# The last eight experts of a mixture of experts add into one target instead of two, and the other sum is added from on chip

## The chip, the core and the metric

The kernel runs on one core of one Trainium2 chip. The core's engines work side by side: PE (TensorE, matmuls and transposes), DVE (VectorE), ACT (ScalarE), POOL (GpSimd) and SP (SyncE), which here only issues transfers. 16 DMA engines move data between HBM and the on-chip memory (SBUF); all transfers share them, whichever engine issues them. The metric is the device time of one execution in microseconds; smaller is better.

## The reference

The program is two layers of gated attention and feed-forward over 4 x 512 tokens of width 512. The change concerns its last part, a mixture of 64 experts: each token takes its best 8 experts, each expert works on at most 128 tokens, and each token's result is the weighted sum over its experts.

```python
x = x + tanh(g_xattn[0]) * L0_xattn(layernorm(x), ctx)
x = x + tanh(g_ffn[0]) * L0_ffn(layernorm(x))
x = x + tanh(g_xattn[1]) * L1_xattn(layernorm(x), ctx)
x = x + tanh(g_ffn[1]) * L1_ffn(layernorm(x))

def L1_ffn(hidden_states):                 # E, K, F, CAP = 64, 8, 192, 128
    scores = softmax(xf @ router_w.T)
    topk_w, topk_idx = top_k(scores, K)
    topk_w = topk_w / (topk_w.sum(-1) + 1e-20)
    xb = buf[:E * CAP].reshape(E, CAP, h)  # each expert's tokens
    gate = einsum('ech,ehf->ecf', xb, w_gate)
    up = einsum('ech,ehf->ecf', xb, w_up)
    yb = einsum('ecf,efh->ech', silu(gate) * up, w_down)
    slot_out = yb[dest] * topk_w
    return zeros((T, h)).at[slot_token].add(slot_out)
```

## The kernel before

The stages of both layers run one after the other. The last, `layer1_ffn`, first runs `route`, which decides for each expert which rows it takes (`slots`, 128 row numbers for each of the 64 experts) and writes a table of normalised token rows with their weights (`token_table`, in HBM). Meanwhile the ring of expert weights is filled: `ring` holds 17 experts (`RING_E`), 6 KB for gate and up and 4 KB for down a partition each, and expert e lies in slot e % 17. `out` already holds x, the residual, 2048 rows of 512 and 128 spare rows; `second` (`second_sum` in the trace, 2176 rows too) is a tensor of the same shape in HBM that was set to zero long before.

`experts` then runs the 64 experts e = 0 .. 63. For each:
- GpSimd gathers the expert's 128 token rows from the table into `xg` (line 2619), four experts ahead (`AHEAD`).
- PE turns them (line 2672), multiplies by gate and up (2682), turns the product h (2690) and multiplies by down (2699); ACT copies and takes the tanh; DVE builds h (2719, 2721).
- DVE scales the result by each row's weight into `yw` (2727), which has four buffers.
- GpSimd scatters `yw` back with an indirect DMA that adds in flight (line 2629): even experts into `out`, odd ones into `second`.

Two adding transfers into the same rows of one tensor must not be in flight together, so a scatter waits for the landing of the previous scatter into the same target, that is the one two experts before (semaphores `scattered[0]` and `scattered[1]`, 16 for each landing). In GpSimd's order expert e has: wait for `scaled`, gather e + 4, wait for the earlier scatter, scatter e. SP loads the weights of expert e (three transfers, lines 2755 and 2756) once expert e - 17 has finished with their slot.

When both targets' last scatters have landed, GpSimd adds `second` to `out` with four adding transfers from HBM to HBM (line 2635), 512 rows of `out` each, in which every one of 128 descriptors is a run of 2048 floats, 8 KB. Then the kernel ends.

Of the kernel before, what the change touches and what calls it, by code (L numbers as in the profile page):

```python
# [13 lines left out]
ALU = mybir.AluOpType  # L14
# [12 lines left out]
D = 512  # L27
KC = D // P
NT = S // P
T = B * S  # L30
# [46 lines left out]
class Stage:  # L77
# [7 lines left out]
    def sb(self, name, shape, dt):  # L85
        return self.ctx.enter_context(self.nc.sbuf_tensor(f"{self.name}_{name}", shape, dt))
# [4 lines left out]
    def sem(self, name):  # L91
        made = self.nc.semaphore(f"{self.name}_{name}")
        if any(word in name for word in self.OF_DMAS):

            self.kept.append(made)
            return made.__enter__()
        self.sems.append(self.ctx.enter_context(made))
        return self.sems[-1]
# [2178 lines left out]
E = 64  # L2277
# [3 lines left out]
OUT_ROWS = T + CAP  # L2281
# [297 lines left out]
AHEAD = 4  # L2579
RING_E = 17  # L2580
PARTS = 4
W_EXPERT = 2 * KC * F1 + 2 * D
SHARED_E = 6


def experts(nc, table, out, second, slots, wgu, wd, w_loaded, load, c):

    with ExitStack() as ctx:
        st = Stage(nc, ctx, "e1")
        sb, ps, sem = st.sb, st.ps, st.sem  # L2590
# [5 lines left out]
        yw = sb("yw", [P, AHEAD, D], F32)  # L2596
# [3 lines left out]
        y_ps = [ps(f"y_ps{i}", [P, D], F32) for i in range(2)]  # L2600
        names = ("x_turned x_copied gu_done tanhed h_begun h_made h_turned h_copied y_done scaled")
        s = {n: sem(n) for n in names.split()}
        sum_stored = sem("sum_stored")
        scattered = [sem(f"scattered{i}") for i in range(2)]
        gathered = [sem(f"gathered{i}") for i in range(AHEAD)]

        with nc.Block() as block:

            @block.sync
            def _(sp):  # L2610
                for e in range(RING_E, E):
                    sp.wait_ge(s["y_done"], e - RING_E + 1)
                    load(sp, e)

            @block.gpsimd
            def _(pool):
                def gather(e):
                    if e < E:
                        pool.indirect_dma_start(xg[:, e % AHEAD], None, table[:],  # L2619
                                                bass.IndirectOffsetOnAxis(ap=slots[:, e:e + 1], axis=0),  # L2620
                                                bounds_check=OUT_ROWS - 1, compute_op=ALU.bypass).then_inc(gathered[e % AHEAD], 16)
                for e in range(AHEAD):
                    gather(e)
                for e in range(E):
                    pool.wait_ge(s["scaled"], e + 1)
                    gather(e + AHEAD)
                    if e >= 2:
                        pool.wait_ge(scattered[e % 2], 16 * (e // 2))
                    pool.indirect_dma_start((out, second)[e % 2][:], bass.IndirectOffsetOnAxis(ap=slots[:, e:e + 1], axis=0), yw[:, e % AHEAD], None,  # L2629
                                            bounds_check=OUT_ROWS - 1, compute_op=ALU.add).then_inc(scattered[e % 2], 16)  # L2630
                for i in range(2):
                    pool.wait_ge(scattered[i], 16 * (E // 2))  # L2632
                for n in range(PARTS):
                    part = [a[n * T // PARTS:(n + 1) * T // PARTS].rearrange("(p t) n -> p (t n)", t=4) for a in (out, second)]
                    pool.dma_start(part[0], part[1], accum_op=ALU.add, max_dma_last_dim=8192).then_inc(sum_stored, 16)  # L2635
                pool.wait_ge(sum_stored, 16 * PARTS)

            @block.scalar
# [73 lines left out]
            @block.vector  # L2712
            def _(dve):
                def inner(e):
                    i = e % 2
                    dve.wait_ge(s["tanhed"], e + 1)
                    if e >= 2:
                        dve.wait_ge(s["h_turned"], e - 1)
                    dve.scalar_tensor_tensor(h[:, i], th[:, i], 1.0, gu_ps[i][:, 0:F1], ALU.add, ALU.mult).then_inc(s["h_begun"], 1)  # L2719
                    dve.wait_ge(s["h_begun"], e + 1)  # L2720
                    dve.scalar_tensor_tensor(h[:, i], h[:, i], 0.5, gu_ps[i][:, F1:2 * F1], ALU.mult, ALU.mult).then_inc(s["h_made"], 1)

                def scale(e):
                    dve.wait_ge(s["y_done"], e + 1)
                    if e >= AHEAD:
                        dve.wait_ge(scattered[e % 2], 16 * ((e - AHEAD) // 2 + 1))
                    dve.tensor_scalar(yw[:, e % AHEAD], y_ps[e % 2][:], xg[:, e % AHEAD, D + e:D + e + 1], None, ALU.mult).then_inc(s["scaled"], 1)  # L2727

                for e in range(E + 1):
                    if e < E:  # L2730
                        inner(e)
                    if e:
                        scale(e - 1)
# [5 lines left out]
def layer1_ffn(nc, d, x_in, out, second, moments, rows_stored, c):  # L2739

    with ExitStack() as ctx:
        st = Stage(nc, ctx, "m1")
        slots = st.sb("slots", [P, E + 2], U32)
        ring = st.sb("ring", [P, RING_E, W_EXPERT], F32)
        wgu = ring[:, :, 0:2 * KC * F1].rearrange("p r (i k f) -> p r i k f", i=2, k=KC)
        wd = ring[0:FP, :, 2 * KC * F1:].rearrange("p r (c n) -> p r c n", c=2)
        w_loaded = [st.sem(f"w_loaded{u}") for u in range(RING_E)]
        table = nc.dram_tensor("token_table", (OUT_ROWS, ROW), F32, kind="Internal").ap()
        gu_src = [d[n].rearrange("e (p k) f -> e p k f", p=P) for n in ("w_gate", "w_up")]
        d_src = d["w_down"].rearrange("e (p c) n -> e p c n", p=FP)  # L2750

        def load(eng, e):
            u = e % RING_E
            for i in range(2):
                eng.dma_start(wgu[:, u, i], gu_src[i][e]).then_inc(w_loaded[u], 16)
            eng.dma_start(wd[:, u], d_src[e]).then_inc(w_loaded[u], 16)

        route(nc, d, x_in, table, out, slots, ring, load, moments, rows_stored, c)
        experts(nc, table, out, second, slots, wgu, wd, w_loaded, load, c)
        st.clear()  # L2760
def rotary_tables():

# [75 lines left out]
```

## Time and profile before

| | us |
|---|---|
| median of 3 runs | 2864.15 |
| lowest and highest run | 2855.6 and 2873.57 |
| profiled execution, its own time | 2868.23 |
| its span in the profile | 2866.4 |

The page of the profile gives these shares over the whole span: PE 2607.9 us busy (91%), its weight loads 2100.1 us, DVE 1695.4 us (59%), ACT 1291.3 us (45%), POOL 857.9 us (30%). They are averages over stages with different limits. The expert stage takes the last 420 us or so. The rows that matter here come from four views: windows (busy time of every engine in a stretch, with the granted clock of TensorE as a fraction of its full 2.4 GHz and the busy share of the 16 DMA engines), the chain of work that ended last (each piece was released by the one above it), the timeline of one engine (start, duration, in brackets the idle time before and what ended it) and the landing times of the DMAs of one line (from issue until the semaphore says that the data has landed). A share of the DMA engines may read a little over 1, since packets overlap.

### The profile page before, as it was taken

What the parts mean: (1) busy time and instruction counts of PE and PEld (TensorE: products, weight loads), DVE (VectorE), ACT (ScalarE), POOL (GpSimd) and SP (SyncE); (2) the same over time, 40 slices, a digit from 0 to 9 for tenths busy, and PEclk for the clock granted to TensorE, in tenths of its full rate; (3) what the DMA queues carried; (4) which work ended last, traced back from release to release, by engine and by line L of the source; (5) the groups of instructions that cost most, each with busy time, mean ns of one, the idle gap of its engine ahead of it and who ended that gap; (6) DMA issues with size and microseconds to landing.
All of it is one profiled execution on the core that took longest, in us unless ns stands there. A gap on an engine that the chain in (4) does not pass through costs nothing. (4 is left out here: it accounts for less than half of the span.)

```text
span 2866.4 us, 48638 instructions
## 1 busy us (share of the span) xinstructions
PE 2607.9 (91%) x17264; PEld 2100.1 (73%) x17291; DVE 1695.4 (59%) x3810; ACT 1291.3 (45%) x3417; POOL 857.9 (30%) x852
## 2 busy tenths in 40 slices
PE   7999987799999899998999999999999983698895
PEld 5666754699998688887888888888888873355552
DVE  6767687834344766665766666667666657222221
ACT  4777776222123444444655555555555541121221
POOL 3344322000000555554322222222222220344443
PEclk9999998799999999999999999999999996899997
DMA  3110022300012555557512421421241118999976
GB/s 137 45 46 24 20 71 64 101 30 16 30 38 90 179 192 188 178 187 240 172 45 88 141 67 53 144 67 48 83 122 45 38 52 280 257 292 287 291 184 112
DMA packets 227279, 340.06 MB, mean 119 GB/s; under 512 B 24801, under 2 KB 111201, under 8 KB 226529
## 3 DMA queue, kind: packets, MB, share of 16 engines
q1 hardware_dynamic: 209728, 293.56, 32.6%
q0 software_dynamic: 14912, 39.85, 6.6%
q10 hardware_dynamic: 2400, 3.55, 0.4%
q8 instruction: 140, 2.29, 0.3%
q14 instruction: 99, 0.80, 0.1%
HBM read 230.56 MB, written 110.53 MB: 119 GB/s over the span
## 5 line engine op out<-in xcount | busy, mean ns | idle before, releaser
L2058 POOL TENSOR_SCALAR a_prob<-a_prob,a_rinv 128x640 f32<-128x640 f32 (+3 forms) x256 | 253.6, 991 | 741.6 <-DVE a_rinv L2220 741.6
L2210 DVE TENSOR_REDUCE a_mx<-a_s_ps 128x1 f32<-128x640 f32 (+3 forms) x256 | 262.1, 1024 | 247.9 <-PE a_s_ps L2130 241.9
L2082 ACT ACTIVATE a_probT<-a_t_ps 128x512 fp32r<-128x512 f32 (+3 forms) x512 | 237.6, 516 | 346.7 <-PE a_t_ps L2138 346.7
L2226 DVE TENSOR_TENSOR a_probT<-a_t_ps,a_probT 128x512 fp32r<-128x512 f32 (+3 forms) x512 | 276.6, 582 | 45.8 <-ACT a_probT L2082 45.1
L2073 ACT ACTIVATE a_prob<-a_s_ps,a_nb,a_rs 128x640 f32<-128x640 f32 (+3 forms) x256 | 267.9, 1047 | 9.6 <-DVE a_nb L2211 9.6
L137 PE MATMUL a_o_ps<-a_probT,a_v 128*128 128x256 f32 x832 | 245.3, 295 | 0.0
L139 PE MATMUL a_o_ps<-a_probT,a_v 128*128 128x256 f32 x832 | 232.6, 280 | 0.0
L138 PE MATMUL a_o_ps<-a_probT,a_v 128*128 128x256 f32 x832 | 232.4, 279 | 0.0
L2138 PE MATMUL a_t_ps<-kept_ident,a_prob 128*128 128x128 f32 x1664 | 225.2, 274 | 2.6 <-POOL a_prob L2058 2.6
L2138 PEld LDWEIGHTS a_t_ps<-kept_ident,a_prob 128*128 128x128 f32 x1664 | 194.2, 141 | 25.7 <-POOL a_prob L2058 3.2
L736 PEld LDWEIGHTS a_bank<-kept_ident,a_prob 128*128 128x128 f32 x1024 | 114.3, 145 | 121.5 <-ACT a_prob L580 94.1
L736 PE MATMUL a_bank<-kept_ident,a_prob 128*128 128x128 f32 x1024 | 164.1, 290 | 41.4 <-ACT a_prob L580 33.4
L580 ACT ACTIVATE a_prob<-a_prob,a_nmax 128x512 f32<-128x512 f32 x256 | 182.2, 717 | 9.1 <-DVE a_nmax L842 9.1
L2719 DVE SCALAR_TENSOR_TENSOR e_h<-e_th,e_gu_ps 128x192 f32<-128x192 f32 x64 | 22.6, 354 | 272.7 <-ACT e_th L2662 272.7
L2682 PE MATMUL e_gu_ps<-m_ring,e_xT 128*128 128x384 f32 x512 | 180.7, 496 | 1.4 <-ACT e_xT L2645 1.4
L1750 ACT ACTIVATE p_sq<-p_bank 128x128 f32<-128x128 f32 x384 | 101.2, 279 | 154.7 <-PE p_bank L139 154.7
L842 DVE CUSTOM_DVE_ANT_0 a_prob<-a_bank,a_mask 128x512 f32<-128x512 f32 x256 | 161.4, 686 | 12.9 <-PE a_bank L720 12.0
L2682 PEld LDWEIGHTS e_gu_ps<-m_ring,e_xT 128*128 128x128 f32 x512 | 99.6, 195 | 86.5 <-issue 35.2
L138 PEld LDWEIGHTS a_o_ps<-a_probT,a_v 128*128 128x128 f32 x832 | 157.0, 189 | 4.9
L137 PEld LDWEIGHTS a_o_ps<-a_probT,a_v 128*128 128x128 f32 x832 | 156.7, 188 | 5.3
L139 PEld LDWEIGHTS a_o_ps<-a_probT,a_v 128*128 128x128 f32 x832 | 156.3, 188 | 0.0
L2619 POOL DMA_INDIRECT e_xg<-token_table,m_slots x64 | 68.1, 1064 | 276.8 <-DVE e_yw L2727 182.8
(307 smaller groups left out, 7136.2 us busy)
## 6 DMA issues: line engine op xcount, KB each, us to landing
m_ring<-in_w_gate SPq DMA_DIRECT2D x64, 384.0 KB, 6.0
m_ring<-in_w_up SPq DMA_DIRECT2D x64, 384.0 KB, 7.5
m_ring<-in_w_down SPq DMA_DIRECT2D x64, 384.0 KB, 10.7
l_q_hi<-p_turned SPq DMA_DIRECT2D x64, 256.0 KB, 2.4
l_q_lo<-p_turned SPq DMA_DIRECT2D x64, 256.0 KB, 2.1
h_split<-l_q_hi SPq DMA_DIRECT2D x62, 256.0 KB, 3.2
h_split<-l_q_lo SPq DMA_DIRECT2D x62, 256.0 KB, 3.8
l_v_hi<-p_vs SPq DMA_DIRECT2D x32, 256.0 KB, 2.2
```

The source lines that it names most:

```text
L137: pe.matmul(out, ll, rh, start=first, stop=False, **kw)
L138: pe.matmul(out, lh, rl, start=False, stop=False, **kw)
L139: return pe.matmul(out, lh, rh, start=False, stop=last, **kw)
L580: act.activation(prob[:, n % RING0], prob[:, n % RING0], ACT.Exp, bias=nmax[:, n % RING0:n % RING0 + 1], scale=-1.0, accum_out=rsum[:, T % ...
L736: mm = pe.transpose(turn_ps[n % 2][:, a * P:a * P + P], prob[:, n % RING0, a * P:a * P + P], c["ident"][:])
L2058: pool.tensor_scalar(prob[:, k % 4, 0:w], prob[:, k % 4, 0:w], rinv[:, k % 4:k % 4 + 1], 1.0, ALU.mult, ALU.mult).then_inc(s["weighted"], 1)
L2073: act.activation(prob[:, k % 4, 0:w], s_ps[:, k % 2, 0:w], ACT.Exp, bias=nb[:, k % 4:k % 4 + 1], scale=rs[:, u, h:h + 1], accum_out=rsum[: ...
L2082: act.activation(probT[0][:, pair % 2, i * 4:i * 4 + n, k % 2], t_ps[i][:, 0:n * P].rearrange("p (m n) -> p m n", n=P), ACT.Copy).then_inc ...
L2138: mm = pe.transpose(t_ps[i][:, m * P:m * P + P], prob[:, k % 4, (i * 4 + m) * P:(i * 4 + m + 1) * P], c["ident"][:])
L2210: step(dve.tensor_reduce(mx[:, k % 4:k % 4 + 1], s_ps[:, k % 2, 0:w], AX.X, ALU.max))
L2226: dve.tensor_tensor(probT[1][:, pair % 2, i * 4:i * 4 + n, k % 2], t_ps[i][:, 0:n * P].rearrange("p (m n) -> p m n", n=P), probT[0][:, pai ...
L2682: mm = pe.matmul(gu_ps[e % 2][:, 0:2 * F1], xT[:, e % 2, k], wgu[:, u, :, k], start=(k == 0), stop=(k == KC - 1))
```

## The change

The experts from 56 on (`ALTERNATING`) all scatter into `out`; `target(e)` names the target and `nth(e)` counts how many scatters went to it before. SP gets two waits and four transfers behind its last weights: once expert 50 has finished and all 28 scatters into `second` have landed, it loads `second` (without its spare rows) into slots 13 to 16 of the ring, viewed as `sums`. GpSimd's last four adding transfers read from `sums` and not from `second`, and wait for the loads too.

```diff
@@ -2579,11 +2579,13 @@
 AHEAD = 4
 RING_E = 17
 PARTS = 4
+ALTERNATING = 56
+SUM_SLOT = 13
 W_EXPERT = 2 * KC * F1 + 2 * D
 SHARED_E = 6
 
 
-def experts(nc, table, out, second, slots, wgu, wd, w_loaded, load, c):
+def experts(nc, table, out, second, slots, wgu, wd, w_loaded, load, c, ring):
 
     with ExitStack() as ctx:
         st = Stage(nc, ctx, "e1")
@@ -2600,7 +2602,17 @@
         y_ps = [ps(f"y_ps{i}", [P, D], F32) for i in range(2)]
         names = ("x_turned x_copied gu_done tanhed h_begun h_made h_turned h_copied y_done scaled")
         s = {n: sem(n) for n in names.split()}
-        sum_stored = sem("sum_stored")
+        sum_stored, sum_loaded = sem("sum_stored"), sem("sum_loaded")
+        sums = ring[:, SUM_SLOT:SUM_SLOT + 4].rearrange("p r n -> p (r n)")[:, 0:PARTS * 4 * D].rearrange("p (c n) -> p c n", c=PARTS)
+
+        def target(e):
+            return 1 if e % 2 and e < ALTERNATING else 0
+
+        def nth(e):
+            return e // 2 if e < ALTERNATING else ALTERNATING // 2 + e - ALTERNATING
+
+        def part(a, n):
+            return a[n * T // PARTS:(n + 1) * T // PARTS].rearrange("(p t) n -> p (t n)", t=4)
         scattered = [sem(f"scattered{i}") for i in range(2)]
         gathered = [sem(f"gathered{i}") for i in range(AHEAD)]
 
@@ -2611,6 +2623,10 @@
                 for e in range(RING_E, E):
                     sp.wait_ge(s["y_done"], e - RING_E + 1)
                     load(sp, e)
+                sp.wait_ge(s["y_done"], ALTERNATING - 5)
+                sp.wait_ge(scattered[1], 16 * (ALTERNATING // 2))
+                for n in range(PARTS):
+                    sp.dma_start(sums[:, n], part(second, n)).then_inc(sum_loaded, 16)
 
             @block.gpsimd
             def _(pool):
@@ -2625,14 +2641,13 @@
                     pool.wait_ge(s["scaled"], e + 1)
                     gather(e + AHEAD)
                     if e >= 2:
-                        pool.wait_ge(scattered[e % 2], 16 * (e // 2))
-                    pool.indirect_dma_start((out, second)[e % 2][:], bass.IndirectOffsetOnAxis(ap=slots[:, e:e + 1], axis=0), yw[:, e % AHEAD], None,
-                                            bounds_check=OUT_ROWS - 1, compute_op=ALU.add).then_inc(scattered[e % 2], 16)
-                for i in range(2):
-                    pool.wait_ge(scattered[i], 16 * (E // 2))
+                        pool.wait_ge(scattered[target(e)], 16 * nth(e))
+                    pool.indirect_dma_start((out, second)[target(e)][:], bass.IndirectOffsetOnAxis(ap=slots[:, e:e + 1], axis=0), yw[:, e % AHEAD], None,
+                                            bounds_check=OUT_ROWS - 1, compute_op=ALU.add).then_inc(scattered[target(e)], 16)
+                pool.wait_ge(scattered[0], 16 * (nth(E - 1) + 1))
+                pool.wait_ge(sum_loaded, 16 * PARTS)
                 for n in range(PARTS):
-                    part = [a[n * T // PARTS:(n + 1) * T // PARTS].rearrange("(p t) n -> p (t n)", t=4) for a in (out, second)]
-                    pool.dma_start(part[0], part[1], accum_op=ALU.add, max_dma_last_dim=8192).then_inc(sum_stored, 16)
+                    pool.dma_start(part(out, n), sums[:, n], accum_op=ALU.add, max_dma_last_dim=8192).then_inc(sum_stored, 16)
                 pool.wait_ge(sum_stored, 16 * PARTS)
 
             @block.scalar
@@ -2723,7 +2738,7 @@
                 def scale(e):
                     dve.wait_ge(s["y_done"], e + 1)
                     if e >= AHEAD:
-                        dve.wait_ge(scattered[e % 2], 16 * ((e - AHEAD) // 2 + 1))
+                        dve.wait_ge(scattered[target(e - AHEAD)], 16 * (nth(e - AHEAD) + 1))
                     dve.tensor_scalar(yw[:, e % AHEAD], y_ps[e % 2][:], xg[:, e % AHEAD, D + e:D + e + 1], None, ALU.mult).then_inc(s["scaled"], 1)
 
                 for e in range(E + 1):
@@ -2756,7 +2771,7 @@
             eng.dma_start(wd[:, u], d_src[e]).then_inc(w_loaded[u], 16)
 
         route(nc, d, x_in, table, out, slots, ring, load, moments, rows_stored, c)
-        experts(nc, table, out, second, slots, wgu, wd, w_loaded, load, c)
+        experts(nc, table, out, second, slots, wgu, wd, w_loaded, load, c, ring)
         st.clear()
 def rotary_tables():
```

The order of instructions changes in two places. The first is GpSimd's end, from the scatter of expert 55 on (`L2629` before is `L2645` now, the gather `L2619` is `L2635`; tiles `e_yw` are the scaled results, `m_slots` the row numbers). Before:

```order
 L2629 DMA second_sum<-e_yw,m_slots 2176x512
 L2619 DMA e_xg<-token_table,m_slots 128x576
 L2629 DMA out_rows<-e_yw,m_slots 2176x512
 L2619 DMA e_xg<-token_table,m_slots 128x576
 L2629 DMA second_sum<-e_yw,m_slots 2176x512
```

Changed:

```order
 L2645 DMA second_sum<-e_yw,m_slots 2176x512
 L2635 DMA e_xg<-token_table,m_slots 128x576
 L2645 DMA out_rows<-e_yw,m_slots 2176x512
 L2635 DMA e_xg<-token_table,m_slots 128x576
 L2645 DMA out_rows<-e_yw,m_slots 2176x512
```

Nothing is moved in GpSimd's stream; every second scatter has another target, and the last four transfers another source.

The second is the end of SP's queue, behind the loads of expert 63 (`m_ring` is the ring):

```order
+L2770 DMA m_ring<-in_w_gate 128x768
+L2770 DMA m_ring<-in_w_up 128x768
+L2771 DMA m_ring<-in_w_down 96x1024
+L2629 DMA m_ring<-second_sum 128x2048 x4
+L2619 UNCONDITIONAL_BRANCH
```

The four loads of the second sum stand last on that queue, with nothing behind them.

## Rows read from the trace of the kernel before

**Rows 1.** windows by stage, core 0; x counts instructions, PEclk is the granted clock

```profile
core 0: us, PE busy (x) PEld busy (x) DVE busy (x) ACT busy (x) POOL busy (x), PEclk, DMA share, GB/s
5.00:25.00 20.00, 14.07 (x56) 11.54 (x57) 12.90 (x22) 8.12 (x11) 4.05 (x5) 1.00 1.04 373
2500.00:2700.00 200.00, 179.49 (x598) 101.96 (x596) 48.10 (x99) 39.95 (x100) 88.60 (x68) 0.97 1.05 289
2752.00:2818.00 66.00, 66.00 (x229) 38.15 (x228) 18.06 (x38) 15.58 (x39) 34.20 (x26) 1.00 0.58 111
2841.00:2861.60 20.60, 0.00 (x0) 0.00 (x0) 0.00 (x0) 0.00 (x0) 0.96 (x2) 0.50 0.95 197
```

**Rows 2.** chain that ended last, its last pieces: start us, us, what

```profile
2821.28 0.48 PE e_x_ps L2672 x4
...
2829.67 2.00 PE e_y_ps L2699 x4
2831.67 0.02 issue
2831.69 0.76 DVE e_yw L2727
...
2833.21 4.68 DMA second_sum<-e_yw,m_slots
2837.89 0.02 issue
2837.91 0.02 POOLq L2632
2837.93 0.56 issue
2838.49 3.47 POOL out_rows L2635 x4
```

**Rows 3.** timeline of GpSimd from 2795 us on: start us, us, line, operation [idle before]

```profile
2795.14 1.59 POOL L2629 DMA_INDIRECT second_sum<-e_yw,m_slots  x1 [0.31 <-issue]
...
2800.39 1.59 POOL L2629 DMA_INDIRECT out_rows<-e_yw,m_slots  x1 [0.31 <-issue]
...
2805.65 1.59 POOL L2629 DMA_INDIRECT second_sum<-e_yw,m_slots  x1 [0.31 <-issue]
...
2814.79 1.06 POOL L2619 DMA_INDIRECT e_xg<-token_table,m_slots  x1 [2.30 <-DVE e_yw L2727]
2816.16 1.59 POOL L2629 DMA_INDIRECT second_sum<-e_yw,m_slots  x1 [0.31 <-issue]
...
2830.56 1.56 POOL L2629 DMA_INDIRECT out_rows<-e_yw,m_slots  x1 [3.72 <-DMA second_sum<-e_yw,m_slots]
2833.21 1.56 POOL L2629 DMA_INDIRECT second_sum<-e_yw,m_slots  x1 [1.09 <-DVE e_yw L2727]
2838.49 3.47 POOL L2635 DMA_DIRECT2D out_rows<-second_sum  x4 [3.72 <-DMA second_sum<-e_yw,m_slots]
```

**Rows 4.** line 2635, the final sum, and the DMA queue in its stretch

```profile
L2635 POOL DMA_DIRECT2D out_rows<-second_sum x4: 932/1328/1783, 2838.5 to 2840.2; - x4
...
DMA to landing us min/median/max: 8.3/14.8/21.3
...
DMA packets 576, 4.19 MB, mean 149 GB/s; under 512 B 64, under 2 KB 64, under 8 KB 64
...
q0 software_dynamic: 576, 4.19, 76.3%
```

**Rows 5.** line 2629, scatters: free (2752 on), then beside the weights (2500 to 2700)

```profile
L2629 POOL DMA_INDIRECT second_sum<-e_yw,m_slots x9: 1559/1589/1590, 2753.1 to 2833.2; - x9
...
DMA to landing us min/median/max: 4.6/4.7/5.6
...
L2629 POOL DMA_INDIRECT out_rows<-e_yw,m_slots x17: 1588/1589/1590, 2506.1 to 2699.4; - x17
...
DMA to landing us min/median/max: 6.8/8.8/10.0
```

**Rows 6.** timeline of SP's queue, its last issue

```profile
2744.28 0.43 SPq L2756 DMA_DIRECT2D m_ring<-in_w_down  x1
```

**Rows 7.** DMA queues from 2500 to 2700 us: packets, MB, share of 16 engines

```profile
q1 hardware_dynamic: 13293, 39.20, 63.2%
q0 software_dynamic: 7439, 18.47, 41.7%
```

**Rows 8.** line 2619, gathers: landing, free (2752 on), then beside the weights

```profile
DMA to landing us min/median/max: 3.4/3.6/4.4
...
DMA to landing us min/median/max: 7.0/7.5/8.7
```

**Rows 9.** DMA queue from 2823 to 2838.3 us, where only scatters move

```profile
q0 software_dynamic: 533, 0.96, 44.8%
```

## The prediction

> **What bounds the kernel now.** I read the page first. Its chain of work that ended last names the expert stage (`experts`), so only what happens there moves the end. Next the windows by stage [rows 1]. From 2500 to 2700 us the expert weights stream in: the DMA engines carry 289 GB/s at a share of 1.05, full. From 2752 to 2818 us PE is busy in all 66.00 us at a granted clock of 1.00 (its 2.4 GHz level) while DMA has fallen to 111 GB/s at 0.58. From 2841 to 2861.6 us no engine computes and the DMA engines run at 0.95: this is the final sum of `second` into `out`. I then followed the chain to the end [rows 2]: PE works back to back until 2831.67, VectorE scales the last expert's rows, GpSimd scatters them at 2833.21, the scatter lands 4.68 us later, and after that GpSimd needs 0.02 + 0.02 + 0.56 = 0.60 us to issue the sum. GpSimd's timeline [rows 3] shows the sum beginning at 2838.49, and in 3.47 us all four parts are issued. The last part issues at about 2840.2 and lands 21.3 us later [rows 4], so at 2861.5; the span ends at 2866.4, 4.9 us behind it. Of these 27.9 us from 2838.49 the moving itself takes 2841 to 2861.6.
>
> So two things could shorten this kernel's tail: the last scatter landing earlier than 2837.89, or the sum taking less than 23.0 us from its issue to its last landing (2838.49 to 2861.5). Each of the two is touched by the change.
>
> **What the change does to the scatters.** Before, even experts add into `out` and odd ones into `second`, and a scatter waits only for the one two before it. From expert 56 on (the scatter at 2800.39 in [rows 3], counted back from expert 63's at 2833.21) all eight go to `out`, and each waits for the landing of the one just before it. It waits in GpSimd's stream, so the gather of a later expert queues behind it too. The order is a chain: landing, 0.60 us, issue, landing. A scatter lands in 4.7 us where nothing but gathers is beside it, and in 8.8 us where the weights stream [rows 5]. A free link is therefore 4.7 + 0.60 = 5.3 us, against PE's pace of 5.25 us an expert (2800.39 to 2805.65, [rows 3]). While PE sets the pace the chain keeps up but has no slack: it can't recover a delay. And it loses what the old order had at the end, where expert 63 was scattered 2.65 us behind expert 62. With all eight links free, the last one lands at 2800.39 + 8 x 4.7 + 7 x 0.60 = 2842.2, **4.3 us** later than 2837.89. That is the floor of the chain's cost.
>
> **What the loads of the second sum add.** SP has issued its last weights at 2744.28 [rows 6] and is idle. It now waits for expert 55's scatter, issued at 2795.14 [rows 3], to land (4.7 us, so 2799.9) and for expert 50's matmuls (long over), and then issues four loads of 1 MB, 4.19 MB in all, from about 2800.4. Their work isn't on the path by itself: the sum waits for them, and they are in by about 2822 at the 196 GB/s that SP's queue moved beside gathers and scatters in the weight stretch (39.20 MB in 200 us [rows 7]). But they run exactly where the chain of scatters begins. The nearest row for a scatter beside a full queue is the 8.8 us of [rows 5], 4.1 us more than free. From 2800.4 to 2822 the chain passes scatters 56, 57 and 58. I count the first and third as half covered (56 is already moving when the loads arrive, 58 outlasts them) and 57 as wholly covered: two links, 2 x 4.1 = 8.2 us. The last scatter then lands at 2842.2 + 8.2 = 2850.4, **12.5 us** later than before. Bounds: nothing beyond the 4.3 us, if the DMA engines' idle 0.42 [rows 1] takes the loads; and at most the whole of the loads' own moving time, 4.19 MB at the full 289 GB/s = 14.5 us, if the scatters stand behind all of it: 4.3 + 14.5 = 18.8 us.
>
> Those loads come in rows of 8 KB, where the weights' packets are 39.20 MB / 13293 = 2.9 KB [rows 7], so one scatter packet may stand behind more bytes than in the row I price by; the 18.8 us bound covers that. The Trainium skill, DMA: Bandwidth & Descriptors, section Queues, rings and completion order, says that each DMA engine goes round its queues packet by packet. By that rule a scatter's eight packets on an engine would each wait for up to one 8 KB packet of SP's; the trace agrees so far that scatters slow from 4.7 to 8.8 us beside 2.9 KB packets. No run so far has 8 KB packets beside a scatter.
>
> **Who else waits.** Gathers queue behind the waiting scatters. In the free stretch a gather lands in 3.6 us, beside the weights in 7.5 us [rows 8]. The gather of expert 63, issued at 2814.79 before, would go behind scatter 58, which by the links above leaves at about 2817; it is then issued at about 2819 and lands between 2823 and 2826, and the transposes of that expert began at 2821.28 [rows 2]. PE loses 2 to 5 us there, perhaps as much again for experts 61 and 62, so expert 63 is scaled by about 2840 instead of 2832.4. The chain wants it only at about 2845. Hidden; if the chain were free (the 4.3 us case), no gather would be late either. VectorE's wait in `scale` is for the scatter four before: expert 63's is for scatter 59, which lands at about 2829, before 2831.67.
>
> **What happens to the final sum.** It moves the same 4.19 MB in the same 512 packets of 8 KB [rows 4]; only the source is SBUF and no longer HBM. No row has an accumulating transfer of such size from SBUF. The nearest are these. The old sum: 197 GB/s in the 20.6 us from 2841 to 2861.6 [rows 1], 4.06 MB. Plain loads at the start: 373 GB/s [rows 1]. A sum at half the rate of a plain load is what reading two operands for each one written gives, and the destination is still read from HBM. If reading is what limits, an SBUF source saves nothing. At the other end stands a drain at the plain 373 GB/s: 4.06 MB in 10.9 instead of 20.6 us, 9.7 us less. The scatters, which do accumulate from SBUF, speak for the first: 533 packets with 0.96 MB took 0.448 of 16 engines in 15.3 us [rows 9], 0.206 us for about 1.8 KB, 8.7 GB/s an engine and no faster than the old sum's 197 / 16 = 12.3. I take **0 us**, and keep 9.7 us for the range.
>
> [...]
>
> **The sum.** Chain +4.3, loads beside it +8.2, final sum 0, issue and end unchanged: +12.5 us. The profiled execution took 2868.2 us with a span of 2866.4; by it the changed kernel has a span of 2879 us. The median of the runs is 2864.15, 4 us under the profiled one; I add to the median: 2864.15 + 12.5 = **2876.7 us**.
>
> **Rivals.**
> - *The sum was bound by HBM, not by the read side.* Before, each byte crossed HBM three times (two reads, a write), 3 x 197 = 591 GB/s; now twice. At the same 591 GB/s the drain is 296 GB/s, 13.7 us, 6.9 us less. With the chain's 12.5 us: 2864.15 + 12.5 - 6.9 = 2869.8 us. For it: nothing in the trace separates the two limits. Against it: the half-rate agreement, and the scatters' slow packets.
> - *The loads disappear in the idle share.* DMA is 0.58 busy, the loads find room, scatters stay near 4.7 us: +4.3 us, 2868.5 us. Against it: four megabytes at once fill 16 engines for over 14 us.
> - *Faster: an add from SBUF drains like a plain transfer.* The place is the final sum, the price 9.7 us. It decides once it saves more than the chain loses: against 12.5 us the drain would have to take 8.1 us, 501 GB/s, which no row reaches; against the floor of 4.3 us anything over 4.06 MB / 16.3 us = 249 GB/s is enough. At 373 GB/s and 4.3 us: 2864.15 + 4.3 - 9.7 = 2858.8 us.
> - *The scatters stand behind all of the loads:* +18.8 us, 2883 us.
>
> **How the numbers follow.** Forecast 0.42, HBM bound 0.22, loads hidden 0.15, faster 0.10, all of the loads 0.11. The range leaves out most of the faster case and a part above the last: 2861 to 2886 us, which also takes in that medians of this kernel move by some 3 us (runs from 2855.6 to 2873.57). The likeliest case alone has 2873 to 2881. One per cent, about what a measurement of this kernel can tell from no change, is 28.6 us. No case reaches that on either side, since the whole tail touched is some 66 us: faster 0.01, same 0.96, slower 0.03.
>
> **What would show it.** In the changed kernel's profile: GpSimd waits at each of the last seven scatters for the DMA of the one before; scatters 56 to 58 land in 7 to 9 us and the later ones in 4.7; the last lands near 2850; the sum takes about 23 us from its issue to its last landing and over 20 us of moving at about 197 GB/s. A last landing near 2842 says that the loads were hidden. A sum of 12 to 16 us says that the source did matter, and the step on the two reads is the wrong one. An end that comes earlier than 2866 us of span would need both.

## The result and the profile after

The changed kernel is slower by a little: a ratio of 1.0047 with a 95% interval of 1.0037 to 1.0057, which is 13.5 us (10.6 to 16.3). The medians of 20 runs each are 2862.8 us before and 2874.8 us after, 12.0 us apart. The profiled execution has a span of 2874.0 us against 2866.4.

Spans of two executions differ by a few us long before the last experts: expert 56's scatter begins at 2796.75 us in the profile after and at 2800.39 before. So below, everything is counted from that scatter's start, in two pieces: to the first issue of the final sum, and from there to the end of the span. Before, these are 38.10 and 27.91 us [rows 3]; after, 50.10 and 27.15 us. Together 77.25 against 66.01: 11.2 us more.

The timeline of GpSimd of the changed kernel (start, duration, line, operation, idle before); `L2645` is the scatter, `L2635` the gather, and the first row is expert 56's scatter:

```profile
2796.75 1.59 POOL L2645 DMA_INDIRECT out_rows<-e_yw,m_slots  x1 [0.31 <-issue]
2800.64 1.06 POOL L2635 DMA_INDIRECT e_xg<-token_table,m_slots  x1 [2.30 <-DVE e_yw L2742]
2807.82 1.59 POOL L2645 DMA_INDIRECT out_rows<-e_yw,m_slots  x1 [6.11 <-DMA out_rows<-e_yw,m_slots]
...
2814.40 1.59 POOL L2645 DMA_INDIRECT out_rows<-e_yw,m_slots  x1 [3.63 <-DVE e_yw L2742]
...
2819.75 1.59 POOL L2645 DMA_INDIRECT out_rows<-e_yw,m_slots  x1 [2.40 <-DMA out_rows<-e_yw,m_slots]
2825.60 1.58 POOL L2645 DMA_INDIRECT out_rows<-e_yw,m_slots  x1 [4.26 <-DVE e_yw L2742]
2831.01 1.56 POOL L2645 DMA_INDIRECT out_rows<-e_yw,m_slots  x1 [3.83 <-DMA out_rows<-e_yw,m_slots]
2836.46 1.56 POOL L2645 DMA_INDIRECT out_rows<-e_yw,m_slots  x1 [3.89 <-DMA out_rows<-e_yw,m_slots]
2841.78 1.56 POOL L2645 DMA_INDIRECT out_rows<-e_yw,m_slots  x1 [3.77 <-DMA out_rows<-e_yw,m_slots]
2846.85 3.60 POOL L2650 DMA_DIRECT2D out_rows<-m_ring  x4 [3.50 <-DMA out_rows<-e_yw,m_slots]
```

Seven scatters follow expert 56's, and the distances are 11.07, 6.58, 5.35, 5.85, 5.41, 5.45 and 5.32 us, then 5.07 to the sum. Before, they were PE's pace of 5.25 us in the main, with 3.93 us between experts 59 and 60 (shown with run 1) and 2.65 us for the last [rows 3]. The first link is far longer than the rest: the one in which SP's loads began.

What a row names in brackets as the end of a wait is inferred. For scatter 58, at 2814.40, it names VectorE, but these are VectorE's scalings of experts 58 and 59:

```profile
2804.37 0.75 DVE L2742 TENSOR_SCALAR e_yw<-e_y_ps,e_xg 128x512 f32<-128x512 f32 x1 [0.38 <-PE e_y_ps L2714]
...
2813.47 0.75 DVE L2742 TENSOR_SCALAR e_yw<-e_y_ps,e_xg 128x512 f32<-128x512 f32 x1 [1.41 <-PE e_y_ps L2714]
```

Expert 58 was scaled by 2805.12, so what scatter 58 waited for last was scatter 57's landing.

Here is SP's queue, with the time from issue to landing of its four loads:

```profile
2796.35 2.09 SPq L2629 DMA_DIRECT2D m_ring<-second_sum  x4
...
DMA to landing us min/median/max: 6.0/11.3/14.7
```

They begin 0.4 us before scatter 56; the last is issued at about 2797.7 and lands 14.7 us later, at 2812.4. The landing times of scatter 56, then of scatter 57:

```profile
DMA to landing us min/median/max: 10.2/10.2/10.2
...
DMA to landing us min/median/max: 5.8/5.8/5.8
```

A free scatter takes 4.7 us, and one beside the weights 8.8 us [rows 5]; scatter 56 took 10.2 us. Scatters from 58 on land in 4.5 to 5.0 us. This piece of the chain that ended last shows what a link is made of:

```profile
2825.60 4.57 DMA out_rows<-e_yw,m_slots
2830.17 0.02 issue
...
2830.29 0.72 issue
2831.01 4.61 DMA out_rows<-e_yw,m_slots
```

From landing to the next scatter's start there are 0.84 us (2830.17 to 2831.01). PE, too, was late once. In the windows, it stands still from 2807.13 to 2809.31 for expert 61's gather, and the 3.96 us behind that run at a granted clock of 0.57, most of them at the 1.2 GHz level:

```profile
core 0: us, PE busy (x) PEld busy (x) DVE busy (x) ACT busy (x) POOL busy (x), PEclk, DMA share, GB/s
...
2807.13:2809.31 2.18, 0.00 (x0) 0.00 (x0) 0.00 (x0) 0.38 (x1) 1.49 (x1) 1.00 1.02 429
2809.31:2813.27 3.96, 3.96 (x8) 2.17 (x9) 0.71 (x2) 0.82 (x2) 1.16 (x2) 0.57 0.95 299
2813.27:2818.50 5.23, 5.23 (x19) 3.04 (x18) 1.46 (x3) 1.20 (x3) 2.65 (x2) 1.00 0.41 62
```

And the final sum: its four issues with the time to landing, and the DMA engines while it moves.

```profile
L2650 POOL DMA_DIRECT2D out_rows<-m_ring x4: 948/1404/1889, 2846.8 to 2848.6; - x4
...
DMA to landing us min/median/max: 7.5/14.0/20.5
...
DMA packets 546, 3.95 MB, mean 201 GB/s; under 512 B 64, under 2 KB 64, under 8 KB 64
```

The time from issue to landing grows by 13.0 us from the first part to the last (7.5 to 20.5), as before (8.3 to 21.3 [rows 4]), with the same spacing of the issues. The drain is the same; every landing, from the first on, comes 0.8 us sooner.

### The profile page after: what moved, and what is told of

It is laid out like the page before. It is cut to its first block and busy times, and to the rows that moved or that the text cites. A ratio compares the mean times of both kernels' runs of the same rounds, so it can differ in the third digit from the quotient of the medians.

```text
span 2874.0 us, 48643 instructions
## 1 busy us (share of the span) xinstructions
PE 2607.3 (91%) x17264; PEld 2101.6 (73%) x17291; DVE 1696.0 (59%) x3810; ACT 1290.3 (45%) x3417; POOL 855.6 (30%) x852
## 5 line engine op out<-in xcount | busy, mean ns | idle before, releaser
L842 DVE CUSTOM_DVE_ANT_0 a_prob<-a_bank,a_mask 128x512 f32<-128x512 f32 x256 | 161.5, 687 | 12.9 <-PE a_bank L720 12.0
L1681 POOL TENSOR_TENSOR p_roped<-p_roped,p_rot 128x512 f32<-128x512 f32 x80 | 102.8, 1285 | 158.6 <-DVE p_rot L1864 158.6
```

## The experiments

Theory A is the one of the prediction: one chain of scatters has no slack against PE, the loads beside it lengthen its first links for good, and an adding transfer gains nothing from an SBUF source. The rivals: the chain keeps up by itself (B), the source matters (C), the loads delay everything by their own moving time whatever stands beside them (D), the loads hurt only by late gathers (E).

| kernel | 56 to sum, us | sum to end, us | both, against before | timed: us (95% interval) |
|---|---|---|---|---|
| before | 38.10 | 27.91 | | |
| changed | 50.10 | 27.15 | +11.2 | +13.5 (10.6 to 16.3) |
| 1 chain only | 45.08 | 28.02 | +7.1 | +4.3 (0.6 to 7.7) |
| 2 source only | 38.24 | 27.56 | -0.2 | 0.0 (-4.3 to 4.3) |
| 3 chain and source, no loads | 45.09 | 27.45 | +6.5 | +6.3 (2.0 to 10.9) |
| 4 loads only | 42.86 | 28.15 | +5.0 | +6.3 (2.3 to 10.0) |
| 5 changed, loads late | 49.76 | 27.29 | +11.0 | +8.9 (4.9 to 12.9) |
| 6 loads only, late | 42.40 | 27.96 | +4.4 | +3.4 (-0.3 to 6.9) |
| 7 changed, loads in 2 KB rows | 52.48 | 27.44 | +13.9 | +9.7 (6.6 to 12.9) |
| 8 changed, chain of four | 47.11 | 27.42 | +8.5 | +5.4 (1.7 to 9.2) |
| 9 loads only, later still | 40.46 | 28.00 | +2.5 | +2.6 (-0.3 to 5.4) |

The timed column is the ratio to the runs of before, less one, times 2863 us. The profile's columns come from one execution each. They leave out how the executions differ earlier, and two kernels were profiled twice up to the sum: run 11, which is run 1's kernel so far, has 44.68 us there (run 1: 45.08), and run 10, which is the changed kernel so far, has 51.14 us (50.10). So differences under about 1 us between two kernels mean little here. In run 7 the profile lies above the timed interval by 1 us.

**1. The chain alone.** The loads are left out and the sum reads HBM as before. This diff and the following ones are against the changed kernel; `...` stands for lines left out.

```diff
-                sp.wait_ge(s["y_done"], ALTERNATING - 5)
-                sp.wait_ge(scattered[1], 16 * (ALTERNATING // 2))
-                for n in range(PARTS):
-                    sp.dma_start(sums[:, n], part(second, n)).then_inc(sum_loaded, 16)
...
-                pool.wait_ge(sum_loaded, 16 * PARTS)
+                pool.wait_ge(scattered[1], 16 * (ALTERNATING // 2))
...
-                    pool.dma_start(part(out, n), sums[:, n], accum_op=ALU.add, max_dma_last_dim=8192).then_inc(sum_stored, 16)
+                    pool.dma_start(part(out, n), part(second, n), accum_op=ALU.add, max_dma_last_dim=8192).then_inc(sum_stored, 16)
```

> The last eight scatters in one chain into out, as in the changed kernel, but no loads of the second sum; the final sum reads HBM as before. Theory A (the chain of scatters has no slack, and the loads beside it add to that): seven links of about 5.4 us behind expert 56's scatter, every landing 4.6 to 5.0 us, the last scatter lands 4 to 6 us later than before relative to expert 56's, time +4 to +6 us. Rival B (only the loads hurt, the chain by itself keeps up with PE): 0 to +2.7 us.

GpSimd's timeline (scatters 56, 57, 63 and the sum), and the landing of the sum's parts:

```profile
2788.70 1.59 POOL L2641 DMA_INDIRECT out_rows<-e_yw,m_slots  x1 [0.31 <-issue]
...
2794.39 1.59 POOL L2641 DMA_INDIRECT out_rows<-e_yw,m_slots  x1 [0.75 <-issue]
...
2828.57 1.56 POOL L2641 DMA_INDIRECT out_rows<-e_yw,m_slots  x1 [4.21 <-DMA out_rows<-e_yw,m_slots]
2833.78 3.47 POOL L2646 DMA_DIRECT2D out_rows<-second_sum  x4 [3.65 <-DMA out_rows<-e_yw,m_slots]
...
DMA to landing us min/median/max: 8.4/14.9/21.4
```

The seven links from scatter 56 to 63 take 39.87 us, 5.70 each, where the prediction had 5.3. The chain that ended last shows landings of 4.79 to 4.93 us and 0.82 to 0.89 us behind each. Before, the same seven steps took 32.82 us, since the pace there wasn't 5.25 us to the end. This row of GpSimd's timeline before is expert 60's scatter, 3.93 us behind expert 59's at 2816.16:

```profile
2820.09 1.58 POOL L2629 DMA_INDIRECT out_rows<-e_yw,m_slots  x1 [2.35 <-DVE e_yw L2727]
```

So the chain loses three things: seven times 0.45 us against PE's pace (3.15 us), the 2.6 us by which expert 63 followed closer on expert 62, and 1.3 us by which the scatters ran earlier from expert 60 on, where no gather stands in front of them any more. Together that is the 7.0 us. B falls by the profile: the chain doesn't keep up. The 4 to 6 us expected were too few there; the timed 4.3 us (0.6 to 7.7) decides neither between 4 and 7 us nor against B.

**2. The source alone.** Scatters alternate to the end, there are no loads, and the sum adds what lies in the ring:

```diff
-            return 1 if e % 2 and e < ALTERNATING else 0
+            return e % 2
...
-            return e // 2 if e < ALTERNATING else ALTERNATING // 2 + e - ALTERNATING
+            return e // 2
...
-                sp.wait_ge(s["y_done"], ALTERNATING - 5)
-                sp.wait_ge(scattered[1], 16 * (ALTERNATING // 2))
-                for n in range(PARTS):
-                    sp.dma_start(sums[:, n], part(second, n)).then_inc(sum_loaded, 16)
...
-                pool.wait_ge(scattered[0], 16 * (nth(E - 1) + 1))
-                pool.wait_ge(sum_loaded, 16 * PARTS)
+                for i in range(2):
+                    pool.wait_ge(scattered[i], 16 * (E // 2))
```

> Scatters alternate to the end as before; only the source of the final sum is SBUF. The loads of the second sum are left out, so the sum adds whatever weights lie in the ring, and the time is that of the source alone. Theory A (the adding transfer is limited by reading two operands, wherever they lie): the sum takes 22.3 us from first issue to last landing as in the changed kernel, against 23.0, time -1.5 to 0 us. Rival C (HBM traffic was the limit, and the gain hides behind the chain in the changed kernel): 16 to 17 us for the sum, time -6 to -7 us.

The sum's issues and its landing times:

```profile
L2646 POOL DMA_DIRECT2D out_rows<-m_ring x4: 948/1401/1884, 2844.0 to 2845.8; - x4
...
DMA to landing us min/median/max: 8.0/14.4/20.9
```

From 8.0 to 20.9 us are 12.9 us: the same drain. Over the runs with an SBUF source the piece from the sum's first issue to the end is 27.15 to 27.56 us, over those with an HBM source 27.91 to 28.15 us. So the source is worth about 0.6 us, none of it in the drain. C falls: it asked for 6 to 7 us, and the timed 0.0 us (-4.3 to 4.3) excludes them too.

**3. Chain and source, no loads.** The changed kernel with the four loads and the wait for them taken out:

```diff
-                sp.wait_ge(s["y_done"], ALTERNATING - 5)
-                sp.wait_ge(scattered[1], 16 * (ALTERNATING // 2))
-                for n in range(PARTS):
-                    sp.dma_start(sums[:, n], part(second, n)).then_inc(sum_loaded, 16)
...
-                pool.wait_ge(sum_loaded, 16 * PARTS)
```

> The changed kernel without its loads (the sum adds what lies in the ring, so the second sum is left out of the result). Theory A: chain +4 to +6 us, sum -0.7 us, in all +3.5 to +5.5 us; the 7 to 8 us that the changed kernel loses beyond that are the loads'. Rival B (the chain keeps up): -1 to +2 us.

45.09 us to the sum, as run 1 with 45.08; the parts add up, and the other 5.0 us of the changed kernel's 12.0 to the sum are the loads'. That is less than the 7 to 8 us that I expected for them, since the chain alone costs more. Run 10, the changed kernel's second profile, puts the loads at 6.1 us (51.14 - 45.09). The first two links show more in the changed kernel: 11.07 and 6.58 us are 6.3 us over two links of 5.70. The later links there, 5.32 to 5.85 us with landings of 4.5 to 5.0 us, are shorter than the 5.70 of the chain alone; nothing in the runs says why.

**4. The loads alone.** Scatters alternate, the sum reads HBM, SP loads x instead of the second sum:

```diff
-            return 1 if e % 2 and e < ALTERNATING else 0
+            return e % 2
...
-            return e // 2 if e < ALTERNATING else ALTERNATING // 2 + e - ALTERNATING
+            return e // 2
...
-                    sp.dma_start(sums[:, n], part(second, n)).then_inc(sum_loaded, 16)
+                    sp.dma_start(sums[:, n], part(x_rows, n)).then_inc(sum_loaded, 16)
...
-                    pool.dma_start(part(out, n), sums[:, n], accum_op=ALU.add, max_dma_last_dim=8192).then_inc(sum_stored, 16)
+                    pool.dma_start(part(out, n), part(second, n), accum_op=ALU.add, max_dma_last_dim=8192).then_inc(sum_stored, 16)
```

> Scatters alternate and the sum reads HBM as before; SP loads four times 1 MB of the program's input x into the same ring slots at the same place as the changed kernel loads the second sum (nothing uses them, so this is extra work). Theory A (the loads hurt because the chain has no slack): alternating scatters have a link of slack each, so only late gathers cost something, 2 to 3 us of PE waiting for e_x_ps; time +1 to +3 us. Rival D (the loads delay everything by their own moving time, whatever the order): +7 us or more.

GpSimd's timeline first (scatter 56, expert 61's gather, the sum), then PE's first row behind its wait, then two windows, PE's wait and the piece behind it:

```profile
2792.89 1.59 POOL L2647 DMA_INDIRECT out_rows<-e_yw,m_slots  x1 [0.31 <-issue]
2796.77 1.06 POOL L2637 DMA_INDIRECT e_xg<-token_table,m_slots  x1 [2.30 <-DVE e_yw L2745]
...
2835.75 3.47 POOL L2653 DMA_DIRECT2D out_rows<-second_sum  x4 [3.87 <-issue]
...
2806.17 0.75 PE L2690 MATMUL e_x_ps<-kept_ident,e_xg 128*128 128x128 f32 x4 [2.91 <-DMA e_xg<-token_table,m_slots]
...
2803.26:2806.17 2.91, 0.00 (x2) 0.00 (x1) 0.00 (x0) 0.38 (x1) 1.34 (x1) 1.00 1.05 364
2806.17:2812.70 6.53, 6.53 (x16) 3.58 (x17) 1.46 (x3) 0.82 (x2) 1.54 (x3) 0.74 0.65 196
```

This cost 4.8 us to the sum's issue, more than the 1 to 3 us that I expected, and it came by another way than in the changed kernel. Gather 61 landed 9.35 us after its issue (2796.77 to 2806.12 in the chain that ended last), PE stood still for 2.91 us, and the next stretch took 1.6 us longer than usual: 6.80 us from one expert's first transpose (2806.17) to the next (2812.97), at a mean granted clock of 0.74 and not 1.00. I had counted the wait but not the clock that falls after it. Rival D asked for 7 us or more here, so by the profile the 5.0 us are neither theory's (the timed interval, 2.3 to 10.0 us, takes in both).

**5 and 6. The loads later.** Both hold the loads back until expert 59 has finished, run 5 in the changed kernel, run 6 in the kernel of run 4:

```diff
-                sp.wait_ge(s["y_done"], ALTERNATING - 5)
+                sp.wait_ge(s["y_done"], 60)
```

> The changed kernel, with its four loads held back until expert 59 has finished, so that all gathers have landed and only the chain of the last scatters is beside them. By the first four runs the chain alone costs 7 us in the profile and the loads 5 us more. Theory A (a scatter slowed by the loads is lost for good, since the chain is slower than PE): the loads cost the same 5 us or so from their new place, one or two of scatters 60 to 62 land in 6 to 10 us; time +10 to +13 us against before. Rival E (the loads cost through late gathers and PE's wait, not through the scatters): with the gathers out of the way only the chain's cost is left, +4 to +7 us.

> Scatters alternate to the end and the sum reads HBM as before; four loads of x as extra work, held back until expert 59 has finished. Theory A (with alternating scatters the loads hurt through the gather alone, which PE waited for by 2.9 us and after which its matmuls ran slower): no gather is left to be late, and a scatter has a link of slack, so 0 to +2 us. Rival D (the loads delay everything by their moving time, whatever stands beside them): +4 us or more.

The premise was wrong by one gather: expert 63's is issued right behind expert 59's end (at 2807.64 in run 5, 2803.33 in run 6), so the loads still caught it; PE waited 1.1 us for it in run 5 and 2.5 us in run 6. Run 5 came out at +11.0 us, as A has it, with one gap of 10.39 us between scatters 59 and 60; so it was scatter 59 that was slowed, not one of 60 to 62. Run 6 missed A's 0 to +2 us: its +4.4 us, 4.3 of them before the sum, look like D's figure, but they come as in run 4, from PE's wait of 2.5 us and a slower stretch behind it (granted clock 0.74 over 6.6 us). Since a gather was beside the loads in both, this pair doesn't separate A from E. Runs 8 and 9 do.

**7. Smaller rows in the loads.**

```diff
-                    sp.dma_start(sums[:, n], part(second, n)).then_inc(sum_loaded, 16)
+                    sp.dma_start(sums[:, n].rearrange("p (t n) -> p t n", t=4), second[n * T // PARTS:(n + 1) * T // PARTS].rearrange("(t p) n -> p t n", p=P)).then_inc(sum_loaded, 16)
```

> The changed kernel, with its loads cut into rows of 2 KB and not 8 KB (the rows then lie at other tokens' places, so the second sum is added to the wrong tokens). Theory A (a scatter's packets each wait behind one packet of the loads): scatter 56, which took 10.2 us in the changed kernel, lands in 7 to 9 us; time 1 to 3 us under the changed kernel's. Rival (the DMA engines share by bytes or are simply full): scatter 56 again above 9.5 us and the same time as the changed kernel, +12 us against before.

The chain that ended last, scatters 56 and 57:

```profile
2795.68 8.58 DMA out_rows<-e_yw,m_slots
...
2805.08 8.61 DMA out_rows<-e_yw,m_slots
```

Scatter 56 landed in 8.58 us and not 10.2, as expected, but scatter 57 then took 8.61 us and not 5.8: together 17.2 against 16.0 us. The profile has the whole 2.7 us above the changed kernel, the timed runs some 4 us under it, and these intervals overlap. So scatter 56 landed sooner beside smaller packets; that the total gets shorter, which I expected too, is not shown. PE also waited here, 3.0 us for expert 62's gather, but the chain hid it. How the packets take turns doesn't by itself give the cost of the loads.

**8. A chain of four.** `ALTERNATING = 60`, and all else as in the changed kernel.

> The changed kernel with the last four experts in one chain and not the last eight; the loads begin when expert 59's scatter has landed. Theory A: the chain loses 0.45 us less on each of four links that are gone (7.0 - 1.8 = 5.2 us), and the loads beside the last four scatters cost about 5 us as before: +9 to +11 us. Rival E (loads hurt through gathers, and none is left): +4 to +6 us.

GpSimd's timeline, scatters 60 to 63 and the sum:

```profile
2818.47 1.58 POOL L2645 DMA_INDIRECT out_rows<-e_yw,m_slots  x1 [2.35 <-DVE e_yw L2742]
2828.70 1.56 POOL L2645 DMA_INDIRECT out_rows<-e_yw,m_slots  x1 [8.65 <-DVE e_yw L2742]
2835.20 1.56 POOL L2645 DMA_INDIRECT out_rows<-e_yw,m_slots  x1 [4.94 <-DMA out_rows<-e_yw,m_slots]
2840.86 1.56 POOL L2645 DMA_INDIRECT out_rows<-e_yw,m_slots  x1 [4.10 <-DMA out_rows<-e_yw,m_slots]
2845.88 3.61 POOL L2650 DMA_DIRECT2D out_rows<-m_ring  x4 [3.46 <-DMA out_rows<-e_yw,m_slots]
```

By 2819.38, when the loads begin, every gather has landed, and no row shows PE waiting for one. The first two links are 10.23 and 6.50 us against 5.7 free: 5.3 us for the loads, with scatter 60 landing after 8.94 us by the chain that ended last. (VectorE had scaled expert 61 by 2822.9, so what scatter 61 waited for was that landing, whatever its row names.) So in the profile the loads cost the same 5 us through the scatters alone, and E falls for a chain. The total of +8.5 us is a little under A's +9 to +11, and the timed +5.4 us (1.7 to 9.2) would suit E as well; what speaks against E is the 10.23 us link with no gather beside it. By difference, the chain of four costs 9.0 - 5.3 = 3.7 us; no run has it without the loads.

**9. The loads alone, later still** (`y_done` 61 in run 4's kernel), so that gather 63 is in.

> As the second run of loads of x beside alternating scatters, but held back one expert more, until expert 60 has finished: expert 63's gather, which the run before still caught, has landed by then. Theory A (alternating scatters absorb the loads, only gathers don't): no wait of PE for a gather; scatters 60 and 61 land in 8 to 10 us and nobody but expert 63's scatter waits for them, 0 to +1 us, the stretch from scatter 60 to the sum's first issue 18.4 to 19.5 us. Rival D (the loads delay everything): +4 to +5 us there.

The chain that ended last, scatters 61 and 63 and the sum:

```profile
2815.63 9.27 DMA second_sum<-e_yw,m_slots
...
2825.71 4.90 DMA second_sum<-e_yw,m_slots
...
2831.20 3.48 POOL out_rows L2653 x4
```

No wait of PE for a gather is left. Scatter 61 took 9.27 us, and since scatter 63 has the same target, it left at 2825.71 instead of about 2823.7. The cost is 2.4 us to the sum, 2.5 in all: half of what the same loads cost a chain (5.3 us), and half of what D gives, so D falls. Alternation absorbs a part, not all; I had expected at most 1 us.

**10 and 11. The last four transfers without the add,** from SBUF in the changed kernel and from HBM in run 1's; the result is then the second sum alone. One execution each:

```diff
-                    pool.dma_start(part(out, n), sums[:, n], accum_op=ALU.add, max_dma_last_dim=8192).then_inc(sum_stored, 16)
+                    pool.dma_start(part(out, n), sums[:, n]).then_inc(sum_stored, 16)
```

> The changed kernel with its last four transfers as plain stores from SBUF into out, without the add (the result is then the second sum alone). Theory A (the adding transfer is limited by reading two operands): the moving takes about half, 10 to 12 us, 350 to 400 GB/s, where the adding one moved at 201 GB/s. Rival C (writes to HBM, or the issue from GpSimd, are the limit): 17 to 20 us.

> The chain of eight scatters without loads, and the last four transfers as plain copies from HBM to HBM, without the add. Theory A: one operand is read, wherever it lies, so the same 10 to 12 us as the plain store from SBUF. Rival C (HBM traffic is the limit): slower than the store from SBUF by a third or more, 15 us or more.

Expert 56's scatter, then issues and landings of the last four transfers of run 10:

```profile
2789.71 1.59 POOL L2645 DMA_INDIRECT out_rows<-e_yw,m_slots  x1 [0.31 <-issue]
...
L2650 POOL DMA_DIRECT2D out_rows<-m_ring x4: 533/556/625, 2840.8 to 2842.6; - x4
...
DMA to landing us min/median/max: 4.4/7.3/10.1
```

Of run 11:

```profile
L2646 POOL DMA_DIRECT2D out_rows<-second_sum x4: 493/520/613, 2834.3 to 2835.9; - x4
...
DMA to landing us min/median/max: 6.0/9.7/13.1
```

From the first issue to the last landing the plain store takes 11.9 us (2840.85 to 2842.6 + 10.1), the plain copy from HBM 14.7 us, the adding transfer 22.3 us. Plain writes and GpSimd's issue are therefore not what limits the sum; the add is. Whether it is the second read or the adding itself that takes the time, no run separates. The copy from HBM is slower than the store from SBUF by 2.8 us, less than C asked for; its packets were also merged into fewer, larger ones, so the 2.8 us are not the source's alone.

The Trainium skill, Collectives: The Full Stack, section on the bandwidth ceiling (the fold count), says of the adding transfers of a collective that both operands are read through the same read ring, so that they run at half a copy's rate. The trace agrees for the SBUF source, 11.9 us without the add and 22.3 us with it, and less closely for HBM, 14.7 and 23.0 us. The page says nothing of the memory that an operand lies in; that the drain is the same from either source, runs 1 and 2 show.

## Why the prediction was right, point by point

The forecast was +12.5 us, 2876.7 us; measured were +12.0 us by the medians and +11.2 us in the profile's tail. The mechanism is as forecast, but that the sum came so close is luck: the chain was put 2.7 us too low, the loads beside it 3.2 us too high, and the two errors cancel.

- **What bounds the kernel: right.** The tail is the last scatter's landing and the sum behind it, in both profiles.
- **The chain's own cost: right in kind, too small.** 4.3 us were forecast, 7.0 measured in runs 1 and 3. The link was sized at 4.7 + 0.60 us and is 4.85 + 0.85. The 0.60 us was read off the sum's issue, which isn't an indirect transfer. The row to read was in [rows 2]: VectorE ended at 2832.45 and the scatter began at 2833.21, 0.76 us later. By it the link would have been 5.5 us. I called the pace of the chain equal to PE's 5.25; it is slower, and seven links make much of that small difference.
- **The loads beside it: right in kind, too large.** 8.2 us were forecast, as two wholly covered links; 5.0 us were measured (50.10 - 45.09), 6.1 us in run 10. The loads ran for 16 us, from 2796.35 to 2812.4, and not for the 21.4 us that 196 GB/s gives. A likely reason, not tested, is that only one scatter and one gather at a time stood beside them. So they covered scatter 56 wholly and scatter 57 in all but its end, and scatter 58 not at all. The excess fell on scatter 56 (10.2 us, against the 8.8 of the weight stretch); scatter 57 took only 5.8 us, though the loads stood beside 4.6 of them, where 8.8 had been put down.
- **PE's wait for gathers: hidden, as forecast, but it came elsewhere.** I had put it on expert 63's gather, queued behind scatter 58, and perhaps those of 61 and 62. PE waited for expert 61's alone, 2.2 us. That gather was issued before the chain held anything back (2800.64) and landed 8.6 us later, beside the loads; then PE ran at a lower clock, which I hadn't counted. Behind the wait expert 59 was scaled by 2814.22. Before, scatter 59 followed the scaling by 2.15 us, so here it could have left at 2816.4; the chain let it go at 2819.75. The wait had some 3.4 us to spare. Run 4 shows the price without the chain as cover: 4.8 us.
- **The final sum: right.** Forecast 0, measured -0.8 us here and -0.6 us over all runs, and a drain that hasn't moved. The rivals that lived on a faster drain, HBM as the limit (-6.9 us) and a plain transfer's rate (-9.7 us), fall by run 2; run 10 shows that a plain store has such a rate and the add takes it away. My reason, two reads for each write, fits but isn't separated from the adding itself.
- **The rival with the loads hidden in the idle share: wrong,** by the changed kernel against run 3, and by run 8. A mean share of 0.58 says how much fits over a stretch, not what a transfer in the middle of it waits.

No version that beats the kernel before came out of this. The only gain in the change is about 0.6 us at the sum's start; the chain that makes the early load possible costs 7.0 us by itself, and by difference 3.7 us even with four experts.

What stays open: why the loads take 5 to 6 us from a chain, most of it from one scatter. Run 4's 4.8 us, from alternating scatters with gathers beside the loads, look like chance in their nearness to it, since each is traced to its own waits, but no run varied the amount loaded.

## What to carry to other kernels

Before work is put into one chain of transfers, compare the link (landing plus the next issue, both read for that kind of instruction) with the pace of whoever feeds it: a chain slower by half a microsecond has no slack, and whatever is moved beside its start is paid for at its end. And ask what an operand brought on chip early would speed up: here the adding transfer drained at the same rate from SBUF as from HBM, and only its start got 0.6 us shorter. A sum that comes out right says little of its terms; check each in a run of its own.

## What the runs showed of the hardware

- From a landing to the start of the waiting indirect scatter 0.81 to 0.89 us pass where the chain shows nothing but the issue between them (the changed kernel, runs 1 and 9); the sum's first direct transfer starts 0.3 us after its landing in the runs with a chain and 0.6 us in the kernel before and run 9.
- PE's waits of 2.18, 2.91, 2.47 and 3.03 us (the changed kernel, runs 4, 6 and 7) were followed by 4 to 8 us at a mean granted clock of 0.57 to 0.74, where the stretches before the wait had 1.00; in run 4 that cost 1.6 us more than the wait. It isn't so after every such wait: after 2.70 us in run 10 and 1.11 us in run 5 the clock stayed at 1.00.
- A scatter of 256 KB beside four megabyte loads landed after 10.2 us with 8 KB rows in the loads (9.9 us in run 10), and after 8.6 us with 2 KB rows (the next scatter too), against 4.85 us free.
- 4.19 MB added into HBM take 22.3 us from SBUF and 23.0 us from HBM; stored without the add from SBUF, 11.9 us.
